# A decoder layer on one core: the columns' load and constants moved behind the first LayerNorm, the table load ahead of the first wait, and three stretches of unread matmuls dropped or cut

## The chip, the cores and the metric

The kernel runs on one NeuronCore of a Trainium2 chip. The metric is the device time of one execution in microseconds (us), lower is better. "PE" is TensorE, "ACT" is ScalarE, "DVE" is VectorE, "POOL" is GpSimd, and "SP" is SyncE, which here only issues transfers.

## The reference

```python
def reference(x, ctx_1024, ...):                      # x, ctx: (32, 128, 256) float32
    x = x + attn(layernorm(x), Wq, bq, Wk, bk, Wv, bv, Wo, bo)   # linear, 16 heads, phi = elu + 1
    x = x + xattn(layernorm(x), ctx, ctx, Wq, Wk, Wv)            # softmax, 16 heads of 16
    x = x + ffn(layernorm(x), w1, w2, h1, h2, w3, ...)           # ternary weights, hidden 1024
    return x

def attn(x, ...):
    q, k, v = phi(x @ Wq.T + bq), phi(x @ Wk.T + bk), x @ Wv.T + bv   # by head
    num = einsum('bhsd,bhsde->bhse', q, cumsum(k[..., :, None] * v[..., None, :], axis=2))
    den = einsum('bhsd,bhsd->bhs', q, cumsum(k, axis=2))
    return (num / (den[..., None] + 1e-6)) @ Wo.T + bo

def ffn(x, ...):
    h = silu(tlin(x, w1_w, w1_s)) * tlin(x, w2_w, w2_s)    # tlin(x, w, s) = (x @ w.T) * s
    h = gelu(tlin(h, h1_w, h1_s)); h = gelu(tlin(h, h2_w, h2_s))
    return tlin(h, w3_w, w3_s)
```

## The kernel before

The 32 sequences are worked on in 16 groups of two (g = 0 to 15, 256 tokens each), and the feed-forward part in 8 blocks of two groups. A planner in Python, run when the program is built, fixes for each engine one list of steps (`ln1T`, `q`, `k`, `xk`, `v`, `xv`, `lin_scores`, and so on); at run time every engine goes through its list in order and waits on semaphores. Nothing in the change alters the planner's tables, so the lists stay as they are.

All transfers of the start are issued by SP on one queue, one behind the other: `x_in` (the first group's input), `cst` (identity, masks), `columns_sb` (38 columns of scales and biases for 128 partitions, 152 bytes to a partition), then the seven weights. After the fifth weight come the context, `bvb`, and then `x_in` for group 1, which waits until the first transposes have read `x_in` (`xn1_turned`); behind it stand `xb`, `bob`, and the weights `woT` and `xqT`.

A weight becomes two parts: ACT copies it to a rounded fp32r part (`split`, L767) and DVE computes the rest (`split`, L934). The first LN1 is: statistics on DVE (L869, L872), the reciprocal root on POOL (`ve`, `rstd`, L706 and L709), normalisation on DVE (L875). PE then transposes the result (`ln1T`, L1058), ACT and DVE split it (L764, L879), and the projections `q` and `k` (L1082, L1087) follow, then `xk`, `v` and `xv` (L1097), where the x stands for the cross attention, which works on the context. ACT takes the exponentials of q and k (L777, L783), DVE makes phi from them (L885, L890), and DVE writes `kz`, k masked by head (L953). PE's `lin_scores` (L1141) needs `kz`; its products are masked on DVE (`lin_mask`, `att_l`, L968) and summed with v on PE (`lin_sums`, L1113); DVE turns the sums (`by_token`, L909) and divides.

The context of a group, `ctx_in`, is rounded by ACT (`ctxs`, L772) and its rest computed by POOL (L734); `xk` of that group waits for both, and ACT's L772 for group 1 waits until `xv` of group 0 is done.

Between these steps PE runs matmuls of the identity with itself, whose results nobody reads. The table FILL says ahead of which step, and how many; they go to the bank that the step will overwrite:

```python
FILL = {("ln1T", 0, 0): 24, ("q", 0, 0): 20, ("xv", 0, 0): 40, ("lin_scores", 0, 1): 20}
```

They need `identb`, the bf16 identity, which ACT makes from `cst` after it has loaded its table of functions (L751, L752).

Of the kernel before, what the change touches and what calls it, by code (L numbers as in the profile page):

```python
# [5 lines left out]
def decoder_layer_program(nc, x, ctxT, wqT, wkT, wvT, woT, bv, bo, xqT, xkT, xvT,  # L6
# [3 lines left out]
    ALU, ACT, AX = mybir.AluOpType, mybir.ActivationFunctionType, mybir.AxisListType  # L10
# [301 lines left out]
    while left:  # L312
        upcoming = []
        for engine in engines:
# [14 lines left out]
            if engine == "tensor" and found:  # L329
# [4 lines left out]
                for entry in found:  # L334
                    step, n = entry[1][1], entry[1][3]
# [27 lines left out]
            if not found:  # L363
                continue
            _, key, when = found[0]
            _, step, g, n = key
            took = tasks[key][1]
            if engine == "tensor":
# [40 lines left out]
    def steps(engine):  # L409
        return [(step, g, n) for _, step, g, n in program[engine]]  # L410
# [13 lines left out]
    def sem(name):  # L424
        return outer.enter_context(nc.semaphore(name))

    with outer:
        flag = outer.enter_context(nc.sbuf_tensor("inexact_flag", [1, 1], I32))
        flag_ready = sem("flag_ready")
        cols = outer.enter_context(nc.sbuf_tensor("columns_sb", [P, 4 * KH + 3 * C], F32))  # L430
        s1c, s2c, sh1c, sh2c = (cols[:, n * KH:(n + 1) * KH] for n in range(4))
        s3c, bqc, bkc = (cols[:, 4 * KH + n * C:4 * KH + (n + 1) * C] for n in range(3))
# [3 lines left out]
        with ctx:  # L436
            def sb(name, shape, dt=F32):
                return ctx.enter_context(nc.sbuf_tensor(name, shape, dt))
# [9 lines left out]
            bq1, bk1 = (sb(n, [P, C]) for n in ("bq1", "bk1"))  # L448
# [17 lines left out]
            v, xv = sb("v", [P, GB, H, 2 * HD]), sb("xv", [P, GB, H, 2 * HD])  # L466
# [22 lines left out]
            s1h, s12 = sb("s1h", [P, KH]), sb("s12", [P, KH])  # L489
# [3 lines left out]
            consts_loaded, cols_loaded = sem("consts_loaded"), sem("cols_loaded")  # L493
            weights = {n: sem(f"{n}_loaded") for n in ("wq", "wk", "wv", "xk", "xv", "wo", "xq", "bv", "bo")}
            ln_const, const_ready, act_const, bias_ready = sem("ln_const"), sem("const_ready"), sem("act_const"), sem("bias_ready")
# [29 lines left out]
            scales = sem("scales_done")  # L525
# [31 lines left out]
            def pbank(step, g, n=0):  # L557
                return bank[place[step, g, n]]

            def wait_pbank(eng, step, g, n=0):  # L560
                if use_before[step, g, n] is not None:
                    wait_freed(eng, *use_before[step, g, n])

            def wait_count(eng, s, count):

                if count > 0:
                    eng.wait_ge(s, count)
# [22 lines left out]
            def _(eng):  # L590
                def load_x(g):
                    wait_count(eng, xn1_turned, g)
                    eng.dma_start(x_in[:, :, :], x[GB * g:GB * g + GB].rearrange("b s d -> s b d")).then_inc(x_loaded, 16)

                def load_xb(g):
                    wait_count(eng, xn2_turned, g)
                    eng.dma_start(xb[:, :, :], x[GB * g:GB * g + GB].rearrange("b s d -> s b d")).then_inc(xb_loaded, 16)

                def load_ctx(g):
                    wait_count(eng, ctx_done, g)  # L600
                    eng.dma_start(ctx_in[:, :, :], ctxT.rearrange("(c p) t -> p c t", p=P)[:, :, T * g:T * g + T])\
                       .then_inc(ctx_loaded, 16)
# [26 lines left out]

                load_x(0)  # L630
                eng.dma_start(cst[:, :], consts).then_inc(consts_loaded, 16)
                eng.dma_start(cols[:, :], columns).then_inc(cols_loaded, 16)
                for n, (dst, src) in enumerate(zip(whole, (wqT, wkT, wvT, xkT, xvT, woT, xqT))):
                    if n == 5:
                        load_ctx(0)
                        eng.dma_start(bvb[:, :], bv.partition_broadcast(P)).then_inc(weights["bv"], 16)
                        load_x(1)
                        load_xb(0)
                        eng.dma_start(bob[:, :], bo.partition_broadcast(P)).then_inc(weights["bo"], 16)
                    eng.dma_start(dst, src.rearrange("(c p) o -> p c o", p=P)).then_inc(weights[SPLIT[n]], 16)  # L640
# [106 lines left out]

            @block.scalar
            def _(eng):
                eng.wait_ge(consts_loaded, 16)  # L750
                eng.preload_act_table(ACT.Exp)  # L751
                eng.activation(identb[:, :], ident, ACT.Copy).then_inc(act_const, 1)  # L752
                eng.wait_ge(cols_loaded, 16)
                eng.activation(s1h[:, :], s1c[:, :], ACT.Copy, scale=0.5).then_inc(scales, 1)
                eng.wait_ge(scales, 1)

                def halves(t):
                    return t[:, :].rearrange("p (c t) -> p c t", c=C)
# [1 line left out]
                for step, g, n in steps("scalar"):  # L760
# [7 lines left out]
                    elif step == "ctx":  # L768
# [2 lines left out]
                        wait_count(eng, xv_psum, g)  # L771
                        eng.activation(ctxs[:, 0, :, :], ctx_in[:, :, :], ACT.Copy).then_inc(ctx_hi, 1)  # L772
                    elif step == "q":
                        eng.wait_ge(q_psum, g + 1)
                        wait_count(eng, kz_done, 2 * g)
                        for c in range(C):
# [89 lines left out]
            def _(eng):  # L866
# [7 lines left out]
                def normalise(ln, which, dst, src, b):  # L874
                    eng.tensor_scalar(dst, src, mv[:, which, b, 0:1], rstd[:, which, b:b + 1], ALU.subtract, ALU.mult)\  # L875
                       .then_inc(ln["xn"], 1)
# [37 lines left out]
                    eng.transpose(out[:, :, :].rearrange("p c (k s) -> p k c s", s=32),  # L914
                                  o[:, :].rearrange("p (k c d) -> p k c d", c=C, d=32)).then_inc(out_turned, 1)

                eng.wait_ge(cols_loaded, 16)
                eng.tensor_scalar(bq1[:, :], bqc[:, :], 1.0, None, ALU.add).then_inc(bias_ready, 1)
                eng.tensor_scalar(bk1[:, :], bkc[:, :], 1.0, None, ALU.add).then_inc(bias_ready, 1)
                eng.scalar_tensor_tensor(s12[:, :], s1c[:, :], 0.5, s2c[:, :], ALU.mult, ALU.mult).then_inc(bias_ready, 1)  # L920
                eng.wait_ge(bias_ready, 3)

                for step, g, n in steps("vector"):
                    if step == "ln1_stats":
# [3 lines left out]
                    elif step == "ln1":  # L928
                        eng.wait_ge(LN1["rstd"], g + 1)
                        for b in range(GB):  # L930
                            normalise(LN1, 0, xn1[:, b, :], x_in[:, b, :], b)
                    elif step == "split":
                        eng.wait_ge(split_hi, g + 1)
                        eng.tensor_tensor(split[g][:, 1, :, :], whole[g], split[g][:, 0, :, :].bitcast(F32), ALU.subtract)\  # L934
# [113 lines left out]
            def _(eng):  # L1048
# [11 lines left out]

                FILL = {("ln1T", 0, 0): 24, ("q", 0, 0): 20, ("xv", 0, 0): 40, ("lin_scores", 0, 1): 20}

                def fill(step, g, n):
                    if (step, g, n) in FILL:
                        first = 4 * n if step in ("lin_scores", "max", "x_scores") else n // 2 if step == "lin_sums" else n
                        wait_pbank(eng, step, g, first)
                        for _ in range(FILL[step, g, n]):
                            eng.matmul(pbank(step, g, first)[:, 0:P], identb[:, :], identb[:, :], start=True, stop=True)  # L1070
# [80 lines left out]
                for step, g, n in steps("tensor"):  # L1151
# [90 lines left out]
                    elif step == "hidden":  # L1242
                        n, quarter = n // 4, n % 4
# [41 lines left out]
        with ctx:  # L1285
# [9 lines left out]
            s1h, s12 = sb("general_s1h", [P, KH]), sb("general_s12", [P, KH])  # L1295
# [244 lines left out]
```

## Time and profile before

| | |
|---|---|
| Median of 3 runs | 1069.11 us (1068.78 to 1071.15) |
| The profiled execution's own time | 1070.74 us |
| Its span in the trace | 1068.9 us |
| PE busy | 1041.0 us, 97% |
| DVE busy | 770.6 us, 72% |
| ACT busy | 528.7 us, 49% |
| POOL busy | 262.1 us, 25% |
| Granted clock of PE over the span | 0.999 |

The page divides the span into 40 slices; PE shows 9 tenths or more in all but the first, where it shows 7. So PE is the engine that the kernel is short of, and the only slice in which it visibly rests is the one that this change is about. A start time in the rows below is counted from the start of the span, and the figure behind it is how long the row lasted.

### The profile page before, as it was taken

Reading aid. Unit: us, or ns where it says so; the run is one execution under the profiler, and the core shown is the slowest. Engines: PE = TensorE matmul, PEld = TensorE weight load, DVE = VectorE, ACT = ScalarE, POOL = GpSimd, SP = SyncE. Lnnn points to the kernel's source line nnn. Section 1 sums busy time; section 2 is a strip of 40 time slices with the busy share of each in tenths; the row PEclk is TensorE's granted clock in tenths of the full one; section 3 lists DMA queues with packets and bytes.
Section 4 is the critical chain, followed back from the end, with each engine's and each line's share of the span. In section 5 each row is a group of like instructions: output and inputs, shape, how many; then the busy total and the mean of one; then the engine's idle time right before and its main releaser. Section 6 shows DMA issues by size and latency. Waiting matters only on the chain.

```text
span 1068.9 us, 25693 instructions
## 1 busy us (share of the span) xinstructions
PE 1041.0 (97%) x10186; PEld 867.0 (81%) x10186; DVE 770.6 (72%) x1708; ACT 528.7 (49%) x855; POOL 262.1 (25%) x363
## 2 busy tenths in 40 slices
PE   7999999999999999999999999999999999999997
PEld 7989877878877888778788878787888888787886
DVE  5999898767996879777898778987688356413321
ACT  4344554855546635555455546374543635333431
POOL 3323352100441115301161011520025002400500
PEclk9999999999999999999999999999999999999999
DMA  5687866443643453543644425453364335545541
GB/s 161 228 285 252 254 230 209 159 138 104 210 148 125 139 166 131 168 136 119 212 137 162 139 86 167 159 147 114 124 231 146 131 125 209 175 142 192 170 155 63
DMA packets 76744, 174.90 MB, mean 164 GB/s; under 512 B 10960, under 2 KB 26448, under 8 KB 76624
## 3 DMA queue, kind: packets, MB, share of 16 engines
q1 hardware_dynamic: 73168, 161.70, 45.1%
q10 hardware_dynamic: 3456, 11.54, 3.9%
q8 instruction: 83, 1.36, 0.5%
q14 instruction: 37, 0.30, 0.1%
HBM read 145.38 MB, written 39.35 MB: 173 GB/s over the span
## 4 chain that ended last, share of the span: by engine, by line
PE 85%; DVE 10%; issue 2%; DMA 2%; ACT 0%; POOL 0%; SPq 0%; ACTq 0%; DVEq 0%
PE bank L1254 43%; PE bank L1141 8%; PE bank L1239 6%; PE bank L1274 6%; PE bank L1113 5%; PE bank L1082 5%; PE bank L1097 3%; PE bank L1087 2%; PE bank L1058 2%; DVE hidden_full L1020 2%; DVE mx L989 1%; DVE hidden_full L1023 1%; PE bank L1191 1%; PE bank L1134 1%; PE bank L1070 1%
## 5 line engine op out<-in xcount | busy, mean ns | idle before, releaser
L1254 PE MATMUL bank<-hidden_a,weight_ring 128*128 128x512 f32 x1024 | 251.4, 396 | 0.0
L1254 PE MATMUL bank<-hidden_b,weight_ring 128*128 128x512 f32 x1024 | 248.0, 395 | 0.3 <-DVE inexact_flag L1045 0.3
L1254 PEld LDWEIGHTS bank<-hidden_b,weight_ring 128*128 128x128 f32 x1024 | 187.7, 188 | 39.4 <-issue 0.8
L1254 PEld LDWEIGHTS bank<-hidden_a,weight_ring 128*128 128x128 f32 x1024 | 187.2, 188 | 40.0 <-issue 1.4
L857 ACT ACTIVATE hidden_full<-bank,columns_sb 128x512 f32<-128x512 f32 x128 | 88.2, 689 | 221.0 <-PE bank L1254 220.6
L706 POOL TENSOR_TENSOR ve<-mv,eps 128x1 f32<-128x1 f32 (+1 forms) x80 | 21.0, 262 | 472.7 <-DVE mv L872 472.7
L1239 PE MATMUL bank<-hidden_b,weight_ring 128*128 128x512 f32 x512 | 123.0, 393 | 1.8 <-DMA weight_ring<-weights_scratch 1.8
L745 POOL TENSOR_TENSOR hidden_a<-hidden_full,hidden_a 128x512 fp32r<-128x512 f32 x64 | 83.1, 1299 | 168.1 <-ACT hidden_a L852 166.9
L1239 PEld LDWEIGHTS bank<-hidden_b,weight_ring 128*128 128x128 f32 x512 | 94.2, 188 | 21.8 <-DMA weight_ring<-weights_scratch 2.2
L1028 DVE TENSOR_TENSOR hidden_a<-hidden_full,hidden_a 128x512 fp32r<-128x512 f32 x64 | 43.6, 683 | 70.4 <-ACT hidden_a L863 70.1
L989 DVE TENSOR_REDUCE mx<-bank 128x4 f32<-128x512 f32 x128 | 80.3, 679 | 16.1 <-PE bank L1141 15.9
L968 DVE TENSOR_TENSOR att_l<-bank,cst 128x512 f32<-128x512 f32 x128 | 80.5, 676 | 9.9 <-PE bank L1141 9.9
L824 ACT ACTIVATE att_x<-bank 128x512 f32<-128x512 f32 x128 | 67.6, 604 | 40.0 <-PE bank L1141 39.8
L1028 DVE TENSOR_TENSOR hidden_b<-hidden_full,hidden_b 128x512 fp32r<-128x512 f32 x64 | 47.3, 743 | 54.3 <-ACT hidden_b L863 54.1
L909 DVE STREAM_TRANSPOSE by_token<-bank 128x512 f32<-128x512 f32 x64 | 45.5, 711 | 39.4 <-PE bank L1113 39.0
L847 ACT ACTIVATE hidden_full<-bank,s1h 128x512 f32<-128x512 f32 x64 | 44.1, 689 | 50.5 <-PE bank L1239 48.7
L730 POOL TENSOR_TENSOR residual<-residual,stats 128x256 f32<-128x256 f32 x64 | 59.3, 949 | 24.4 <-DMA stats<-stats_scratch 23.1
L1274 PE MATMUL bank<-hidden_a,weight_ring 128*128 128x512 f32 x256 | 64.3, 398 | 0.0
L1274 PEld LDWEIGHTS bank<-hidden_a,weight_ring 128*128 128x128 f32 x256 | 46.4, 188 | 9.5 <-issue 0.2
L852 ACT ACTIVATE hidden_a<-hidden_full 128x512 fp32r<-128x512 f32 x64 | 40.2, 628 | 24.8 <-DVE hidden_full L1023 24.6
L1023 DVE SCALAR_TENSOR_TENSOR hidden_full<-bank,s,hidden_full 128x512 f32<-128x512 f32 x64 | 48.1, 751 | 2.3
L709 POOL TENSOR_TENSOR rstd<-ve,mhalf 128x1 f32<-128x1 f32 (+1 forms) x80 | 48.1, 601 | 6.3
(135 smaller groups left out, 1696.5 us busy)
## 6 DMA issues: line engine op xcount, KB each, us to landing
weight_ring<-weights_scratch SPq DMA_DIRECT2D x160, 512.0 KB, 3.8
weights_scratch<-in_h ACTq DMA_DIRECT2D x16, 512.0 KB, 5.0
xn3T_scratch<-hidden_b SPq DMA_DIRECT2D x16, 512.0 KB, 4.3
weight_bits<-in_h SPq DMA_DIRECT2D x32, 256.0 KB, 3.7
weight_ring<-weights_scratch SPq DMA_DIRECT2D x32, 256.0 KB, 2.7
values_scratch<-hidden_full SPq DMA_DIRECT2D x14, 512.0 KB, 4.8
xv<-values_scratch SPq DMA_DIRECT2D x14, 512.0 KB, 4.7
x_in<-in_x SPq DMA_DIRECT2D x16, 256.0 KB, 3.3
```

Of the source, the lines that this page charges most:

```text
L730: last = eng.tensor_tensor(half[:, c], half[:, c], (sd, mean)[n], (ALU.mult, ALU.add)[n])
L745: eng.tensor_tensor(HA[:, 1, n, :], full[:, n % NFULL, :], HA[:, 0, n, :].bitcast(F32), ALU.subtract)\
L824: eng.activation(att_x[:, (NU * g + n) % NX, :, :], pbank("x_scores", g, n)[:, :].rearrange("p (j s) -> p j s", j=4), ACT.Exp, scale=SCALE ...
L857: eng.activation(full[:, (KH + n) % NFULL, :], pbank("hidden", g, n)[:, :], ACT.Gelu, scale=sc).then_inc(h_full, 1)
L968: eng.tensor_tensor(att_l[:, (NU * g + n) % NL, :, :], pbank("lin_scores", g, n)[:, :].rearrange("p (j s) -> p j s", j=4), causal.rearrang ...
L989: eng.tensor_reduce(mx[:, b, 4 * r:4 * r + 4], pbank("max", g, n)[:, :].rearrange("p (j t) -> p j t", j=4), AX.X, ALU.max).then_inc(max_do ...
L1023: eng.scalar_tensor_tensor(f_, pbank("gate", g, 2 * n + 1)[:, :], s12[:, n:n + 1], f_, ALU.mult, ALU.mult)\
L1028: eng.tensor_tensor(dst[:, 1, m, :], full[:, (KH + n) % NFULL, :], dst[:, 0, m, :].bitcast(F32), ALU.subtract)\
L1141: mm = eng.matmul(pbank(step, g, 4 * b + r)[:, j * S:(j + 1) * S], stationary(rows, e, m, b), moving(rows, e, m, b), start=not shifted, st ...
L1239: mm = eng.matmul(pbank(step, g, n)[:, :], ring[:, n // 4, at_:at_ + P], HB[:, part, kk, :], start=(kk == 0 and part == 0), stop=(kk == C ...
L1254: mm = eng.matmul(pbank(step, g, n)[:, :], ring[:, slot, kk * P:(kk + 1) * P], src[:, part, kk, :], start=(kk == 0 and part == 0), stop=(k ...
L1274: mm = eng.matmul(pbank(step, g, c)[:, :], ring[:, slot, kk % 4 * P:(kk % 4 + 1) * P], HA[:, part, kk, :], start=(kk == 0 and part == 0), ...
```

## The change

The load of the columns is issued after the first two weights. ACT loads its table before it waits for `cst`, and makes `s1h` (half of a column scale, read much later by the tanh) only ahead of the first `q`. DVE makes `bq1`, `bk1` and `s12` from the columns after the first LN1's normalisation. Of the unread matmuls, those ahead of `xv` and of the second `lin_scores` are left out, and the others cut from 24 to 22 and from 20 to 14.

```diff
                 load_x(0)
                 eng.dma_start(cst[:, :], consts).then_inc(consts_loaded, 16)
-                eng.dma_start(cols[:, :], columns).then_inc(cols_loaded, 16)
                 for n, (dst, src) in enumerate(zip(whole, (wqT, wkT, wvT, xkT, xvT, woT, xqT))):
+                    if n == 2:
+                        eng.dma_start(cols[:, :], columns).then_inc(cols_loaded, 16)
...
-                eng.wait_ge(consts_loaded, 16)
                 eng.preload_act_table(ACT.Exp)
+                eng.wait_ge(consts_loaded, 16)
                 eng.activation(identb[:, :], ident, ACT.Copy).then_inc(act_const, 1)
-                eng.wait_ge(cols_loaded, 16)
-                eng.activation(s1h[:, :], s1c[:, :], ACT.Copy, scale=0.5).then_inc(scales, 1)
-                eng.wait_ge(scales, 1)
...
                     elif step == "q":
+                        if g == 0:
+                            eng.wait_ge(cols_loaded, 16)
+                            eng.activation(s1h[:, :], s1c[:, :], ACT.Copy, scale=0.5).then_inc(scales, 1)
+                            eng.wait_ge(scales, 1)
                         eng.wait_ge(q_psum, g + 1)
...
-                eng.wait_ge(cols_loaded, 16)
-                eng.tensor_scalar(bq1[:, :], bqc[:, :], 1.0, None, ALU.add).then_inc(bias_ready, 1)
-                eng.tensor_scalar(bk1[:, :], bkc[:, :], 1.0, None, ALU.add).then_inc(bias_ready, 1)
-                eng.scalar_tensor_tensor(s12[:, :], s1c[:, :], 0.5, s2c[:, :], ALU.mult, ALU.mult).then_inc(bias_ready, 1)
-                eng.wait_ge(bias_ready, 3)
+                def biases():
+                    eng.wait_ge(cols_loaded, 16)
+                    ...
+                    eng.wait_ge(bias_ready, 3)
...
                             normalise(LN1, 0, xn1[:, b, :], x_in[:, b, :], b)
+                        if g == 0:
+                            biases()
...
-                FILL = {("ln1T", 0, 0): 24, ("q", 0, 0): 20, ("xv", 0, 0): 40, ("lin_scores", 0, 1): 20}
+                FILL = {("ln1T", 0, 0): 22, ("q", 0, 0): 14}
```

On DVE, at the start of its list, stood this in the kernel before (`stats`, `mv`: LN1's statistics; `x_in` written from itself: the normalisation; `wq`: the rest of the first weight):

```order
L918 TENSOR_SCALAR bq<-columns_sb 128x2
L919 TENSOR_SCALAR bk<-columns_sb 128x2
L920 SCALAR_TENSOR_TENSOR s<-columns_sb 128x8
L869 BN_STATS stats<-x_in 128x6
...
L872 BN_AGGR mv<-stats 128x2
L934 TENSOR_TENSOR wq<-att_x,wq 128x512
L875 TENSOR_SCALAR x_in<-x_in,mv,rstd 128x256 x2
L934 TENSOR_TENSOR wk<-att_x,wk 128x512
```

Now the same place reads:

```order
L871 BN_STATS stats<-x_in 128x6
...
L874 BN_AGGR mv<-stats 128x2
L939 TENSOR_TENSOR wq<-att_x,wq 128x512
L877 TENSOR_SCALAR x_in<-x_in,mv,rstd 128x256 x2
L921 TENSOR_SCALAR bq<-columns_sb 128x2
L922 TENSOR_SCALAR bk<-columns_sb 128x2
L923 SCALAR_TENSOR_TENSOR s<-columns_sb 128x8
L939 TENSOR_TENSOR wk<-att_x,wk 128x512
```

The three column instructions went from the head of the list to a place behind the normalisation, but the first weight's rest still stands between the statistics and the normalisation.

On PE, from the first `k` of the cross attention to the second `lin_scores`, stood this (a row of `identb` is unread matmuls; `att_l,v` is `lin_sums`):

```order
L1087 MATMUL bank<-ctxs,xwk 128x256 x2
L1097 MATMUL bank<-wv,xn1T 128x256 x12
L1070 MATMUL bank<-identb 128x128 x40
L1097 MATMUL bank<-xwv,ctxs 128x256 x12
L1141 MATMUL bank<-qf,kz 128x128 x16
...
L1113 MATMUL bank<-att_l,v 32x128 x16
L1070 MATMUL bank<-identb 128x128 x20
L1141 MATMUL bank<-qf,kz 128x128 x16
```

Now it reads:

```order
L1092 MATMUL bank<-ctxs,xwk 128x256 x2
L1102 MATMUL bank<-wv,xn1T 128x256 x12
L1102 MATMUL bank<-xwv,ctxs 128x256 x12
L1146 MATMUL bank<-qf,kz 128x128 x16
...
L1118 MATMUL bank<-att_l,v 32x128 x16
L1146 MATMUL bank<-qf,kz 128x128 x16
```

Two rows of unread matmuls are gone; each was directly ahead of a step that waits for other engines too.

## Rows read from the trace of the kernel before

**Rows 1.** Chain that ended last, start of the span: start, length, what.
```profile
1.26 2.62 DMA cst<-in_consts
...
3.88 1.28 ACT L751
...
5.63 2.72 PE bank L1070 x24
8.35 0.94 PE bank L1058 x4
9.29 2.05 PE bank L1070 x20
...
17.05 2.25 PE bank L1070 x40
19.30 1.49 PE bank L1097 x12
...
26.93 1.22 PE bank L1070 x20
```

**Rows 2.** Timeline of DVE, first 10 us; in brackets idle time before and its releaser.
```profile
4.68 0.17 DVE L918 TENSOR_SCALAR bq<-columns_sb 128x2 f32<-128x2 f32 x1 [4.68 <-DMA columns_sb<-in_columns]
...
5.02 0.43 DVE L869 BATCH_NORM_STATS2 stats<-x_in 128x6 f32<-128x256 f32 x1
...
7.39 0.73 DVE L875 TENSOR_SCALAR x_in<-x_in,mv,rstd 128x256 f32<-128x256 f32 x2
...
9.96 0.69 DVE L879 TENSOR_TENSOR xn1T<-bank,xn1T 128x512 fp32r<-128x512 f32 x1 [0.63 <-ACT xn1T L764]
```

**Rows 3.** Timeline of POOL, whole start; same columns.
```profile
6.62 0.72 POOL L709 TENSOR_TENSOR rstd<-ve,mhalf 128x2 f32<-128x2 f32 x1
...
22.00 1.30 POOL L734 TENSOR_TENSOR ctxs<-ctx_in,ctxs 128x512 fp32r<-128x512 f32 x1 [4.38 <-ACT ctxs L772]
```

**Rows 4.** Timeline of SP's queue: when a transfer was issued.
```profile
1.76 0.42 SPq L632 DMA_DIRECT2D columns_sb<-in_columns  x1
2.23 0.43 SPq L640 DMA_DIRECT2D att_x<-in_wqT  x1
```

**Rows 5.** DMA issues of the first 16 us: count, KB, us from issue to landing.
```profile
att_x<-in_wqT SPq DMA_DIRECT2D x1, 256.0 KB, 3.8
...
x<-in_woT SPq DMA_DIRECT2D x1, 256.0 KB, 4.3
```

**Rows 6.** Timeline of ACT, first 30 us.
```profile
12.85 0.84 ACT L777 ACTIVATE ex<-bank,columns_sb 128x256 f32<-128x256 f32 x2 [1.37 <-PE bank L1087]
15.11 0.63 ACT L767 ACTIVATE wo<-x 128x512 fp32r<-128x512 f32 x1 [1.41 <-DMA x<-in_woT]
15.64 0.82 ACT L783 ACTIVATE ex<-bank,columns_sb 128x256 f32<-128x256 f32 x2
```

**Rows 7.** Timeline of DVE, 16 to 80 us.
```profile
16.64 0.42 DVE L885 TENSOR_SCALAR ex<-ex 128x512 f32<-128x512 f32 x1
...
19.15 0.88 DVE L953 TENSOR_SCALAR kz<-ex,cst 128x512 f32<-128x512 f32 x2
...
27.00 0.72 DVE L909 STREAM_TRANSPOSE by_token<-bank 128x512 f32<-128x512 f32 x1 [1.97 <-PE bank L1113]
...
72.84 0.42 DVE L980 TENSOR_TENSOR x<-bank,xb 128x256 f32<-128x256 f32 x1 [0.46 <-PE bank L1194]
```

**Rows 8.** Timelines of POOL and DVE, where the two meet.
```profile
35.71 1.29 POOL L734 TENSOR_TENSOR ctxs<-ctx_in,ctxs 128x512 fp32r<-128x512 f32 x1
35.79 1.69 DVE L875 TENSOR_SCALAR x_in<-x_in,mv,rstd 128x256 f32<-128x256 f32 x2
```

**Rows 9.** Timeline of PE: places where it waited.
```profile
23.36 0.50 PE L1087 MATMUL bank<-ctxs,xwk 128*128 128x256 f32 x2 [0.42 <-POOL ctxs L734]
...
43.09 1.17 PE L1141 MATMUL bank<-qf,kz 32*128 32x128 f32 x32 [0.92 <-issue]
...
984.95 9.36 PE L1239 MATMUL bank<-hidden_b,weight_ring 128*128 128x512 f32 x40 [1.79 <-DMA weight_ring<-weights_scratch]
```

More of the change, by code:

```diff
@@ L749, in _ @@
             def _(eng):
+                eng.preload_act_table(ACT.Exp)
                 eng.wait_ge(consts_loaded, 16)
-                eng.preload_act_table(ACT.Exp)
                 eng.activation(identb[:, :], ident, ACT.Copy).then_inc(act_const, 1)
-                eng.wait_ge(cols_loaded, 16)
-                eng.activation(s1h[:, :], s1c[:, :], ACT.Copy, scale=0.5).then_inc(scales, 1)
-                eng.wait_ge(scales, 1)
                 def halves(t):
@@ L915, in turn_and_divide @@
                                   o[:, :].rearrange("p (k c d) -> p k c d", c=C, d=32)).then_inc(out_turned, 1)
-                eng.wait_ge(cols_loaded, 16)
-                eng.tensor_scalar(bq1[:, :], bqc[:, :], 1.0, None, ALU.add).then_inc(bias_ready, 1)
-                eng.tensor_scalar(bk1[:, :], bkc[:, :], 1.0, None, ALU.add).then_inc(bias_ready, 1)
-                eng.scalar_tensor_tensor(s12[:, :], s1c[:, :], 0.5, s2c[:, :], ALU.mult, ALU.mult).then_inc(bias_ready, 1)
-                eng.wait_ge(bias_ready, 3)
+                def biases():
+                    eng.wait_ge(cols_loaded, 16)
+                    eng.tensor_scalar(bq1[:, :], bqc[:, :], 1.0, None, ALU.add).then_inc(bias_ready, 1)
+                    eng.tensor_scalar(bk1[:, :], bkc[:, :], 1.0, None, ALU.add).then_inc(bias_ready, 1)
+                    eng.scalar_tensor_tensor(s12[:, :], s1c[:, :], 0.5, s2c[:, :], ALU.mult, ALU.mult).then_inc(bias_ready, 1)
+                    eng.wait_ge(bias_ready, 3)
                 for step, g, n in steps("vector"):
```

## The prediction

> **What bounds the kernel now.** I read the page first: PE is busy for 97% of the span, and only the first slice shows it resting. So the second view was the chain of work that ended last, in order of time, over the first 60 us [rows 1]. It is on PE almost throughout, and before 30 us it has four stretches of L1070, the unread matmuls: 2.72, 2.05, 2.25 and 1.22 us. The reader is to see that these look like time that can be had back, 8.2 us in all, and that this is only so where nothing else would have held PE. The third view was the timeline of each engine over the same time, where the brackets tell what each idle engine waited for. DVE rests for the last time at 27.00, where it waits for `lin_sums`; from there to 72.4 it has work without a break [rows 7], and PE waits instead, for 0.92 us at 43.09 [rows 9]. That sets the measure of everything below: the change is worth what it moves the DVE row at 27.00. Later both engines hand the lead to each other, and no time in the program is absolute, so a shift there should reach the end.
>
> **Change part by part.**
>
> *The table load.* ACT waits for `cst` until 3.88, loads for 1.28 us, and only then copies `identb`; PE starts at 5.63 [rows 1]. With the load ahead of the wait it falls into idle time, the copy starts at 3.90, and PE starts at 5.63 - 1.28 = 4.35.
>
> *LN1.* The statistics could not start before 5.02, because the columns' three instructions, waiting for a landing at 4.68, stood ahead [rows 2]. From 5.02 to the end of `rstd` at 7.34 [rows 3] are 2.32 us. `x_in` is the first transfer and `cst`, issued behind it, has landed at 3.88, so the statistics start by 3.9 and `rstd` is there by 6.2. This is no longer what counts: the rest of `wq` stands between statistics and normalisation. `wqT` was issued at 2.23 and landed 3.8 us later, at 6.03 [rows 4, 5]; from there to the normalisation at 7.39 are 1.36 us of copy and rest. It now takes the columns' place at 1.76. With the same 3.8 it lands at 5.56. The columns are 128 pieces of 152 bytes ahead of it in the queue; if they held it up besides, it lands earlier, and I bound that by 0.35 us, which is less than a whole issue (0.42). So LN1 is normalised from 6.57 to 6.92 on and done 0.73 later, at 7.3 to 7.65, against 8.12.
>
> *The transposes.* 22 unread matmuls at 2.72/24 = 0.113 us each end at 6.85, so PE waits 0.5 to 0.8 us for LN1 before the transposes. They begin at 7.35 to 7.7 and, with 0.94 as before, end at 8.3 to 8.65 against 9.29. That is a shift of 0.65 to 1.0; I take 0.8. The columns' three instructions, 0.3 us on DVE behind the normalisation, cost nothing: DVE waited 0.63 us there for ACT [rows 2], and without that cover they would cost their 0.3. `s1h`, a copy of 8 columns, is at most the 0.4 us that one of the two q exponentials of 256 takes, on ACT in a wait of 1.37 us for q [rows 6]; equally free.
>
> *q to xv.* 14 unread matmuls at 2.05/20 give 1.45 us, so q begins at 9.95 instead of 9.29 + 2.05 = 11.34: a shift of 1.4. Nothing on PE waited between there and 17.05, so v ends at 15.65, and without the 40 matmuls `xv`, 1.49 us, ends at 17.15 instead of 19.30 + 1.49 = 20.79 [rows 1].
>
> *Where the 2.25 us go.* `lin_scores` needs `kz`. Follow it back: `kz` ended at 19.15 + 0.88 = 20.03; the chain ahead of it on DVE starts with L885 at 16.64 [rows 7], which needs ACT's k exponential, done at 16.46, which stands in ACT's list behind the copy of `wo`, which waited 1.41 us for the transfer of `woT` [rows 6]. That transfer is issued behind the `x_in` of group 1, which waits for the transposes, and takes 4.3 us [rows 5]. So this chain moves by the transposes' 0.8, not by PE's 1.4, and DVE's slack of 0.15 adds to it: `kz` ends at 19.1. PE will stand idle from 17.15 to 19.1, almost all that the 40 matmuls had filled. `lin_scores` moves from 20.79 to 19.1, by 1.7. Behind it, `xk` of group 1 waited 0.42 us for POOL's `ctxs` [rows 9]; that chain (ACT's `xv` copy, L772, L734) now ends near 19.8, well ahead, so the wait goes and with it some of the slow matmuls about it: 0.4 to 0.65, I take 0.5. DVE's row at 27.00 moves by 2.2.
>
> *What comes late next.* POOL's `ctxs` rest, 1.30 us from 22.00 [rows 3], moves to about 18.5 to 19.8, because its ACT chain follows the k exponential too. Before, it lay beside masking from PSUM. Now it lies beside `kz` and group 1's normalisation, 18.2 to 19.9 on DVE. What that does is seen elsewhere: two normalisations took 1.69 us beside POOL [rows 8] where the first group's took 0.73 [rows 2], ending only after POOL's instruction had. If the second `kz` half is caught, it ends about 0.8 later, and `lin_scores` with it; if only the normalisation is caught, the transposes of group 1 wait some 0.3. I charge 0.4, between the two. The Trainium skill (SBUF — State Buffer, the reading of its diagram) says that VectorE and GpSimd share one port pair as an exclusive lock, so that the loser blocks for the whole instruction. The trace agrees (1.69 against 0.73); without that rule the sum would be 2.2, with it between 1.4 and 1.9.
>
> *The last stretch*, 1.22 us at 26.93, is worth nothing: behind 27.00 DVE leads, and PE's 0.92 wait at 43.09 becomes 2.1.
>
> Sum: 0.8 + 0.15 + 0.75 (PE was that much later than `kz`) + 0.5 - 0.4 = 1.8 us. Against the profiled execution's own 1070.74 (its span is 1068.9) that makes 1068.9, but this execution lay 1.6 above the median of the runs shown; against 1069.11 it makes 1067.3.
>
> **Rivals.**
> 1. *No clash with POOL, or `wqT` lands early.* The sum is then 2.2 to 3.1: 1066.0 to 1066.9. For it: POOL's start depends on three ACT instructions, and 0.1 us decides who is first. Against it: either DVE instruction is in POOL's way.
> 2. *The gain is lost on the way.* Either the clock rises later still (it has a rest of 0.8 us and fewer matmuls to go by), so that PE itself brings `kz` late: a rise at 13 costs 1.5 on PE and leaves 0.7; or DVE and POOL meet more often between 27 and 72. Gain 0 to 1.2: 1067.9 to 1069.1.
> 3. *Slower: the clock falls in the new rest.* PE will rest 1.9 to 2.7 us from 17.15, after a short start. From `lin_scores` to the end of `lin_sums` it has 5.5 us of work; at half speed that is up to 5.5 more. From 1.8 us of it at the low clock on, the change loses; at worst it gives 1069.1 + 3.7 = 1072.8. Against it: after a rest of 1.79 us at 984.95, matmuls of 512 columns went on at 9.36/40 = 0.234 each [rows 9], the fast pace. But that was after long work, and the rest will be longer. The Trainium skill (TensorE: Matmul & The Clock Gate, What's actually happening) says that throttled is the default state and activity is what lifts it; by that rule leaving out filler ahead of a rest speaks for this rival, and the four rows of L1070 are the trace's only witness.
>
> **How the numbers follow.** Forecast, gain 1.3 to 2.2: 0.45. Rival 1: 0.27. Rival 2: 0.18. Rival 3: 0.10. Two tenths of a per cent, 2.1 us, is about what a measurement of this kernel tells from no change (the three runs span 2.4). Faster by more is rival 1 and the upper quarter of the forecast: 0.39; slower by more is rival 3 and a little: 0.11; the rest, 0.50, lies within. The range runs from rival 1's 1065.9 to rival 2's end with the runs' scatter, 1069.4, and leaves out rival 3 and the tails.
>
> **What would show it.** `identb` near 3.9 and the first L1070 near 4.35; the normalisation near 6.7; transposes near 7.5 with PE idle some 0.6 before; `wo` on ACT near 14.3; PE idle about 1.9 us before the first `lin_scores` near 19.1 to 19.9; `by_token` near 25.2 with DVE busy behind it; and a POOL `ctxs` row that overlaps a long `kz` or `x_in` row. I am wrong if matmuls behind 17 us take the slow pace, or if the row at 25.2 has moved but the end has not.

## The result, and the profile after

| | before | after |
|---|---|---|
| Median | 1069.60 us (16 executions) | 1075.15 us (16 executions, 1072.67 to 1079.16) |
| Profiled execution, its span | 1070.74, 1068.9 | 1075.01, 1073.2 |
| Granted clock of PE, mean over the span | 0.999 | 0.995 |
| PE busy | 1041.0 | 1042.5 |

The change makes the kernel slower: after to before is 1.0044, 95% interval 1.0032 to 1.0055, or 4.7 us where 1.8 of gain were forecast. Rival 3, which had a chance of 0.10, is what happened, and it happened twice; the median lies above even its worst case, 1072.8.

First the granted clock. This is PE in the stretches about the two rests in the kernel after; the columns are the stretch, its length, PE's busy time with its instructions, the granted clock, DMA's share and GB/s.

```profile
17.00:19.00 2.00, 0.84 (x8) 1.00 0.00 0
19.00:21.00 2.00, 1.17 (x32) 1.00 0.00 0
21.00:22.00 1.00, 0.86 (x5) 0.51 0.27 71
22.00:23.00 1.00, 1.00 (x7) 0.50 0.59 192
23.00:24.00 1.00, 1.00 (x7) 0.50 0.45 90
24.00:25.00 1.00, 1.00 (x8) 0.78 0.49 172
...
44.00:45.00 1.00, 0.64 (x20) 0.96 0.92 375
45.00:46.00 1.00, 1.00 (x21) 0.50 0.81 271
46.00:47.00 1.00, 1.00 (x5) 0.50 0.19 66
47.00:48.00 1.00, 1.00 (x6) 0.50 0.00 1
48.00:49.00 1.00, 1.00 (x9) 0.84 0.00 0
```

Twice the pace halves, from 2.4 to 1.2 GHz, for 3.4 us each time. Adding up what is missing from 1.00 gives 0.49 + 0.50 + 0.50 + 0.22 = 1.7 us in the first and 0.04 + 3 x 0.50 + 0.16 = 1.7 in the second.

Now PE's own timeline of the kernel after; a bracket is how long PE was idle ahead of the row, and for what.

```profile
4.24 2.50 PE L1075 MATMUL bank<-identb 128*128 128x128 bf16 x22 [4.24 <-ACT identb L753]
7.95 1.12 PE L1063 MATMUL bank<-cst,x_in 128*128 128x128 f32 x4 [1.20 <-DVE x_in L877]
8.86 1.70 PE L1075 MATMUL bank<-identb 128*128 128x128 bf16 x14
10.31 0.93 PE L1087 MATMUL bank<-xn1T,wq 128*128 128x256 f32 x4
...
16.27 1.57 PE L1102 MATMUL bank<-xwv,ctxs 128*128 128x256 f32 x12
19.57 1.17 PE L1146 MATMUL bank<-qf,kz 32*128 32x128 f32 x32 [1.73 <-issue]
21.14 1.12 PE L1063 MATMUL bank<-cst,x_in 128*128 128x128 f32 x4 [0.40 <-DVE x_in L877]
21.91 1.20 PE L1087 MATMUL bank<-ctxs,xwk 128*128 128x256 f32 x4
...
38.18 0.72 PE L1087 MATMUL bank<-ctxs,xwk 128*128 128x256 f32 x4
...
44.36 1.63 PE L1146 MATMUL bank<-qf,kz 32*128 32x128 f32 x32 [2.49 <-issue]
```

The same four matmuls of `xk` take 1.20 us at 21.91 and 0.72 at 38.18. The rests ahead of the two `lin_scores` are 1.73 and 2.49 us; before, PE had filler ahead of the first and rested 0.92 at the second [rows 9].

The other engines of the kernel after, DVE, ACT and POOL, in the same columns, at the rows that answer to [rows 2, 3, 6, 7]:

```profile
6.55 0.69 DVE L939 TENSOR_TENSOR wq<-att_x,wq 128x512 fp32r<-128x512 f32 x1 [1.89 <-ACT wq L765]
7.16 0.73 DVE L877 TENSOR_SCALAR x_in<-x_in,mv,rstd 128x256 f32<-128x256 f32 x2
...
19.39 1.70 DVE L877 TENSOR_SCALAR x_in<-x_in,mv,rstd 128x256 f32<-128x256 f32 x2
...
27.20 0.72 DVE L911 STREAM_TRANSPOSE by_token<-bank 128x512 f32<-128x512 f32 x1 [3.13 <-PE bank L1118]
...
42.34 1.92 DVE L958 TENSOR_SCALAR kz<-ex,cst 128x512 f32<-128x512 f32 x2
...
5.89 0.63 ACT L765 ACTIVATE wq<-att_x 128x512 fp32r<-128x512 f32 x1 [1.79 <-DMA att_x<-in_wqT]
...
14.68 0.63 ACT L765 ACTIVATE wo<-x 128x512 fp32r<-128x512 f32 x1 [1.55 <-DMA x<-in_woT]
...
5.09 0.71 POOL L710 TENSOR_TENSOR rstd<-ve,mhalf 128x2 f32<-128x2 f32 x1
...
19.07 1.54 POOL L735 TENSOR_TENSOR ctxs<-ctx_in,ctxs 128x512 fp32r<-128x512 f32 x1 [2.00 <-ACT ctxs L770]
...
42.40 1.57 POOL L735 TENSOR_TENSOR ctxs<-ctx_in,ctxs 128x512 fp32r<-128x512 f32 x1 [4.29 <-ACT ctxs L770]
```

`by_token`, on which the sum was put, comes at 27.20 with 3.13 us of idle DVE ahead of it, where 27.00 and 1.97 stood [rows 7]: the early start is gone by then. The last two POOL rows each run beside a DVE row that takes twice its usual time.

One of the 16 executions had a mean clock of 0.999, as before, and was the shortest, 1072.67 us. It has no trace, but it suggests that a part of the loss against 1069.60 stays without a fall of the clock.

### The profile page after: what moved, and what is told of

The parts are those of the page before. It is cut to its first block, busy times and chain, and to the rows that moved or that the text cites. A ratio compares the mean times of both kernels' runs of the same rounds, so it can differ in the third digit from the quotient of the medians.

```text
span 1073.2 us, 25557 instructions
## 1 busy us (share of the span) xinstructions
PE 1042.5 (97%) x10118; PEld 866.7 (81%) x10118; DVE 774.4 (72%) x1708; ACT 528.2 (49%) x855; POOL 262.4 (24%) x363
## 4 chain that ended last, share of the span: by engine, by line
PE 80%; DVE 12%; issue 3%; DMA 3%; ACT 1%; POOL 0%; SPq 0%; ACTq 0%; DVEq 0%
PE bank L1259 43%; PE bank L1146 8%; PE bank L1279 5%; PE bank L1118 5%; PE bank L1244 5%; PE bank L1087 4%; PE bank L1102 3%; PE bank L1092 2%; PE bank L1063 2%; DVE hidden_full L1025 2%; DVE mx L994 2%; DVE hidden_full L1028 1%; DMA weight_ring<-weights_scratch 1%; PE bank L1196 1%; PE bank L1139 1%
## 5 line engine op out<-in xcount | busy, mean ns | idle before, releaser
L1244 PEld LDWEIGHTS bank<-hidden_b,weight_ring 128*128 128x128 f32 x512 | 94.2, 188 | 21.4 <-DMA weight_ring<-weights_scratch 1.9
L731 POOL TENSOR_TENSOR residual<-residual,stats 128x256 f32<-128x256 f32 x64 | 59.0, 944 | 25.5 <-DMA stats<-stats_scratch 24.3
```

The source lines that it names most:

```text
L731: last = eng.tensor_tensor(half[:, c], half[:, c], (sd, mean)[n], (ALU.mult, ALU.add)[n])
L1244: mm = eng.matmul(pbank(step, g, n)[:, :], ring[:, n // 4, at_:at_ + P], HB[:, part, kk, :], start=(kk == 0 and part == 0), stop=(kk == C ...
```

## The experiments

Twelve kernels, all run in the same manner beside the kernel before, profiled once each. Their results together; "rest 1" and "rest 2" are PE's idle time in the profiled execution right ahead of the first `lin_scores` of group 0 (near 20 us) and of group 1 (near 44), "low" means that the granted clock fell to 0.5 behind it.

| kernel | median us | ratio to before (95%) | rest 1 | rest 2 |
|---|---|---|---|---|
| after | 1075.15 | 1.0044 (1.0032 to 1.0055) | 1.73 low | 2.49 low |
| head_only | 1070.99 | 1.0011 (0.9998 to 1.0023) | 0.50 | 0.87 |
| fills_only | 1076.23 | 1.0056 (1.0041 to 1.0070) | 2.87 low | 2.57 low |
| xv_back | 1072.67 | 1.0024 (1.0010 to 1.0039) | none | 2.57 low |
| ls_back | 1071.98 | 1.0015 (1.0003 to 1.0026) | 3.08 low | 0.96 |
| both_back | 1069.76 | 0.9982 (0.9971 to 0.9994) | none | 0.94 |
| rests_filled | 1071.60 | 1.0010 (0.9999 to 1.0020) | 1.10 | 0.35 |
| start_long | 1070.56 | 0.9991 (0.9977 to 1.0005) | 2.90 low | 0.78 |
| no_meeting | 1074.01 | 1.0033 (1.0022 to 1.0045) | 2.01 | 2.48 |
| half_fills | 1070.53 | 0.9998 (0.9984 to 1.0012) | 0.69 | 2.37 low |
| norm_first | 1066.57 | 0.9965 (0.9951 to 0.9979) | none | 0.95 |
| weights_late | 1064.95 | 0.9951 (0.9933 to 0.9970) | 1.19 | 0.85 |
| kz_free | 1070.39 | 1.0000 (0.9989 to 1.0011) | none | none |

**The change in two halves.** head_only has the change's loads and order with the unread matmuls of before; fills_only has the old order with the changed table.

```diff
 # head_only, against the kernel after
-FILL = {("ln1T", 0, 0): 22, ("q", 0, 0): 14}
+FILL = {("ln1T", 0, 0): 24, ("q", 0, 0): 20, ("xv", 0, 0): 40, ("lin_scores", 0, 1): 20}
 # fills_only, against the kernel before
-FILL = {("ln1T", 0, 0): 24, ("q", 0, 0): 20, ("xv", 0, 0): 40, ("lin_scores", 0, 1): 20}
+FILL = {("ln1T", 0, 0): 22, ("q", 0, 0): 14}
```

> The changed kernel with all four stretches of unread matmuls as before (24, 20, 40, 20); only the loads and constants are moved. Theory A (the clock falls in rests that the unread matmuls had filled): no stretch below a granted clock of 1.00 behind the first 12 us, DVE's first by_token at 25.5 to 26.5 instead of 27.20, and 1 to 2 us below the kernel before, near 1068. Theory B (what was lost is lost to POOL: PE runs ahead, POOL's rest of the context comes earlier and blocks kz and the normalisation): the earlier start alone still brings these meetings, and the time is 2 us or more above the kernel before.

> The kernel before with only the unread matmuls changed (22, 14, none, none). Theory A: the rest ahead of the first lin_scores is about 1.5 to 2 us and that ahead of the second group's lin_scores about 2 us, the granted clock reads 0.5 behind at least one of them, and the time is 3 to 6 us above before. Theory B: no clock below 1.00, kz of the second group about 1.9 us, the time 1 to 3 us above.

The loss is all in the table: with it alone the kernel takes 1.0056, with the rest alone 1.0011. In fills_only the clock is low from 24.1 to 27.5 and from 48.0 to 51.5. But head_only did not bring the gain of 1 to 2 us that was expected of it. Its trace has no fall before PE's last work, and `by_token` is at 28.02, not at 25.5 to 26.5: PE rests 1.22 us ahead of the transposes, the slow pace lasts to about 13.4, and `kz` begins at 21.33, where it began at 19.15 before.

**Each stretch put back.** The three entries keep 22 and 14 and add one or both of the others.

```diff
-FILL = {("ln1T", 0, 0): 22, ("q", 0, 0): 14}
+FILL = {("ln1T", 0, 0): 22, ("q", 0, 0): 14, ("xv", 0, 0): 40}                              # xv_back
+FILL = {("ln1T", 0, 0): 22, ("q", 0, 0): 14, ("lin_scores", 0, 1): 20}                      # ls_back
+FILL = {("ln1T", 0, 0): 22, ("q", 0, 0): 14, ("xv", 0, 0): 40, ("lin_scores", 0, 1): 20}    # both_back
```

> The changed kernel with the 40 unread matmuls ahead of xv put back. Theory A: the low clock from 21.0 to 24.3 goes, the one from 45.0 to 48.3 stays; by_token near 25.5, and of the 5.5 us lost some 2 come back: 1072 to 1073.5. Theory B: these 40 stand well before the meeting at 42.3, which stays; no more than 0.5 us comes back.

> The changed kernel with the 20 unread matmuls ahead of the second lin_scores put back. Theory A: the rest ahead of lin_scores of the second group falls from 2.5 to some 1.3 us, the clock stays up there, while the first low stretch at 21.0 remains: 1071 to 1073. Theory B: PE is 1.2 us later in front of POOL's rest, kz of the second group is back at 0.9 us, and all of the loss but 1 us is gone, whatever the clock does.

> The changed kernel with both later stretches (40 ahead of xv, 20 ahead of the second lin_scores) put back, the first two left at 22 and 14. Theory A (each low stretch costs on its own): neither the clock at 21 nor that at 45 falls, both parts come back, 1070 to 1071, level with the kernel before. If the first two stretches mattered for the falls, one of them is still there and the time stays at 1072 or more.

Each of the first two removes one of the two low stretches and leaves the other. With both back the change is a gain of 0.18%, 1.9 us. That it is the size of the forecast is luck: two of the forecast's terms, 0.75 and 0.5, came from `xv` without the 40 matmuls, which stand here again. Nor does the trace show where the gain arises: the transposes begin at 8.26 (8.18 before), and `by_token` is at 26.91, 0.09 ahead of before. The 20 matmuls that the prediction held to be worth nothing are worth 1.0044 - 1.0015, 3.1 us, when put back alone. ls_back changes two things near 44 us at once, though: the clock holds, and `kz` takes 0.88 where it took 1.92. So it does not tell these two apart. Its rest 1 is 3.08 where after has 1.73, and 1.0 of that is another `kz`, the first one: it took 1.88 us (19.11) beside POOL's `ctxs` (19.31).

**Only the rests filled.** Unread matmuls are put where PE rests, ahead of the two `lin_scores`, where none had stood.

```diff
+FILL = {("ln1T", 0, 0): 22, ("q", 0, 0): 14, ("lin_scores", 0, 0): 32, ("lin_scores", 1, 0): 40}
```

> The changed kernel with unread matmuls where its trace shows PE resting: 32 behind xv, directly ahead of the first lin_scores (rest of 1.73 us), and 40 directly ahead of the second group's first lin_scores (rest of 2.49 us); none ahead of xv and of the second lin_scores. Theory A: they stand in time that is lost anyway, the clock holds through both places, and xv with POOL's chain behind it is early: 1067.5 to 1069.5, below the kernel before. Theory B: the meetings with POOL are as in the changed kernel (kz of the second group 1.9 us), so 1.5 us or more of the loss stays: 1072 or more.

No clock falls behind them, and 3.6 us come back (1.0044 to 1.0010), about the 3.4 that the low rows add up to. The trace shows it directly: from the first `lin_scores` to `by_token` are 5.57 us here (21.63 to 27.20) and 7.63 in after (19.57 to 27.20), where 0.40 of it is PE's wait for the long normalisation. The time, 1071.6, lies between what the two theories had expected. For 1.0010 is not 0.9982: something besides the clock was lost. In this trace both `kz` are long, the first (19.59) with 1.94 us and the one near 42 with 2.01.

**A longer start.** More matmuls at the start, so that the first rise of the pace comes sooner and no rest stands ahead of the transposes.

```diff
+FILL = {("ln1T", 0, 0): 34, ("q", 0, 0): 20, ("xv", 0, 0): 40, ("lin_scores", 0, 1): 20}
```

> The changed kernel with 34, 20, 40 and 20 unread matmuls: all of the kernel before, and 10 more in the new rest of 1.2 us ahead of the first transposes. Theory A': with only the old numbers the clock first rose at 13.3 instead of 11.1, because of that rest, and this ate the earlier start; now PE works without a rest from 4.3 on, the first rise is at or before 11, and the time is 1 to 2 us below the same kernel with 24: 1068 to 1069.5. Rival: the first rise comes when it comes, whatever PE did in that rest, and the time is as with 24 (1071).

The start went as meant, with the fast pace from about 7.9 us (the transposes at 8.06 took 0.66 us, where after has 1.12), and yet the clock fell behind rest 1, and stayed low for 6.8 us, twice as long as elsewhere. Two thirds of that rest are a transfer's, and the last 1.0 us is POOL's. ACT, DVE and POOL in this run:

```profile
10.81 0.20 ACT L774 ACTIVATE s1h<-columns_sb 128x8 f32<-128x8 f32 x1
11.52 0.84 ACT L779 ACTIVATE ex<-bank,columns_sb 128x256 f32<-128x256 f32 x2 [0.51 <-PE bank L1092]
16.36 0.63 ACT L765 ACTIVATE wo<-x 128x512 fp32r<-128x512 f32 x1 [4.00 <-DMA x<-in_woT]
16.89 0.82 ACT L785 ACTIVATE ex<-bank,columns_sb 128x256 f32<-128x256 f32 x2
...
20.27 1.92 DVE L958 TENSOR_SCALAR kz<-ex,cst 128x512 f32<-128x512 f32 x2
...
20.61 1.28 POOL L735 TENSOR_TENSOR ctxs<-ctx_in,ctxs 128x512 fp32r<-128x512 f32 x1 [4.39 <-ACT ctxs L770]
```

k's exponential stands behind the copy of `wo`, and `woT` took 6.2 us here (4.3 before [rows 5]). PE had finished the filler and `xv` long before and waited for `kz`, which took 1.92 us beside POOL's `ctxs`. Its twelve times fall apart into six from 1068.14 to 1069.35 and six from 1071.76 to 1073.04, the profiled one among the latter, with mean clocks of 0.998 to 0.999 in the first and 0.996 to 0.998 in the second.

**POOL kept out of the first normalisation's way.** In the kernel after, POOL's `ctxs` of group 1 (19.07) runs beside group 1's normalisation (19.39, 1.70 us).

```diff
                     elif step == "ctx":
                         eng.wait_ge(ctx_hi, g + 1)
+                        if g == 1:
+                            eng.wait_ge(LN1["xn"], 2 * GB)
```

> The changed kernel, but POOL's rest of the context of group 1 waits until DVE has normalised that group. Theory A: x_in's normalisation is back at 0.73 us and the 0.40 us rest ahead of the transposes goes, but the rest of 1.73 us ahead of lin_scores and the two low stretches stay: 1074 to 1075.5, at most 0.8 us better. Theory B: this meeting starts the loss: 1072 or less.

The normalisation takes 0.73 us again (20.09). The median gains 1.2 us (1.0044 to 1.0033), and the intervals overlap. Its profiled execution, with 1071.99 the lowest of the twelve, shows no fall of the clock behind rests of 2.01 and 2.48; the other eleven go up to 1076.62 with mean clocks of 0.995 to 0.997. They have no traces, but by these means one and the same rest seems to be followed by a fall in most executions, and not in all.

**Half of the filler.**

```diff
+FILL = {("ln1T", 0, 0): 22, ("q", 0, 0): 14, ("xv", 0, 0): 20, ("lin_scores", 0, 1): 10}
```

> The changed kernel with half of what it left out: 20 unread matmuls ahead of xv and 10 ahead of the second lin_scores. The rests of PE ahead of the two lin_scores should be 1.1 and 0.6 us shorter than in the changed kernel, so about 0.7 and 1.9 us. Theory (a rest of the length seen there, 1.7 to 3.1 us, lets the pace fall; a short one does not): the first stretch at the low clock (21 to 25 us) does not come, the second, behind a rest of 1.9, may; 1070.5 to 1073. Rival (it is the number of matmuls left out, or the short start, not the rest, that counts): both stretches stay and the time is within 1 us of the changed kernel's 1075. If both are gone, the time is about that with both put back whole, 1069.8.

Rest 1 shrinks to 0.69 and the clock holds there. Rest 2 stays long, since DVE leads there and `kz` is late (1.90 us beside POOL), and the clock falls.

**The normalisation ahead of the first weight's rest.** On top of both_back, DVE's list has its normalisation in front of the rest of `wq`.

```diff
-                for step, g, n in steps("vector"):
+                dve_steps = list(steps("vector"))
+                early = next(t for t in dve_steps if t[0] == "ln1" and t[1] == 0)
+                dve_steps.remove(early)
+                at = next(i for i, t in enumerate(dve_steps) if t[0] == "split")
+                dve_steps.insert(at, early)
+                for step, g, n in dve_steps:
```

(`biases()` moves from the normalisation to behind the first `split`.)

> The changed kernel with 40 and 20 unread matmuls put back, and on DVE the first LN1's normalisation ahead of the rest of wq instead of behind it (the columns' three instructions stay behind wq's rest). If the transposes waited for wq's transfer by way of that rest, as I now read it, the normalisation starts near 5.6 instead of 7.5, the transposes near 6.9 instead of 8.3 with no rest before them, and everything to the first lin_scores moves by what woT's landing allows, 0.5 to 1.3 us: 1068.5 to 1069.5, ratio 0.997 to 0.998. Rival: as in the run with a longer start, woT lands no earlier though it is issued earlier, kz stays near 19.3 and the rest ahead of lin_scores becomes long enough for the pace to fall: 1070.5 to 1072.

The gain is larger than expected. DVE and PE in this kernel:

```profile
5.94 0.73 DVE L877 TENSOR_SCALAR x_in<-x_in,mv,rstd 128x256 f32<-128x256 f32 x2 [1.17 <-POOL rstd L710]
6.62 0.69 DVE L942 TENSOR_TENSOR wq<-att_x,wq 128x512 fp32r<-128x512 f32 x1
...
25.07 0.72 DVE L911 STREAM_TRANSPOSE by_token<-bank 128x512 f32<-128x512 f32 x1 [1.95 <-PE bank L1123]
...
6.73 1.12 PE L1068 MATMUL bank<-cst,x_in 128*128 128x128 f32 x4
```

The normalisation no longer waits for `wqT`, in this kernel or in the next (5.94 and 5.86). The transposes follow the 22 matmuls without a rest, and `by_token` is at 25.07, 1.9 ahead of before.

**`wo` and `xwq` out of the way.** As norm_first, and the copies and rests of these two weights stand behind group 1's `ctxs` on ACT and behind group 1's normalisation on DVE. The 40 matmuls ahead of `xv` are left out again, the 20 stay.

```diff
+                late = [t for t in act_steps if t[0] == "split" and t[1] in (5, 6)]
+                act_steps = [t for t in act_steps if t not in late]
+                at = next(i for i, t in enumerate(act_steps) if t[0] == "ctx" and t[1] == 1)
+                act_steps[at + 1:at + 1] = late
...
-FILL = {("ln1T", 0, 0): 22, ("q", 0, 0): 14, ("xv", 0, 0): 40, ("lin_scores", 0, 1): 20}
+FILL = {("ln1T", 0, 0): 22, ("q", 0, 0): 14, ("lin_scores", 0, 1): 20}
```

> As norm_first, and besides the copies and rests of wo and xwq stand behind the context copy of group 1 on ACT and behind group 1's normalisation on DVE, and the 40 unread matmuls ahead of xv are left out (the 20 ahead of the second lin_scores stay). Theory (PE's rest ahead of the first lin_scores is ACT waiting for woT in front of k's exponential): ACT's k exponential starts right behind q's, kz ends near 17, lin_scores follows xv near 17.3 with a rest under 0.6 us, and there is no low clock behind it; by_token moves from 27.2 to about 25, the end to 1067 to 1068.5. Rival A (leaving out the 40 lets the pace fall by itself): a low clock near 20 to 24 us though the rest is short, 1070 to 1073. Rival B (POOL or the masks are late next): kz early, by_token within 0.5 us of 27, 1069 to 1070.

ACT, PE and DVE in this kernel:

```profile
13.09 0.84 ACT L790 ACTIVATE ex<-bank,columns_sb 128x256 f32<-128x256 f32 x2 [1.47 <-DVE qf L897]
...
14.59 1.52 PE L1116 MATMUL bank<-xwv,ctxs 128*128 128x256 f32 x12
17.30 1.17 PE L1160 MATMUL bank<-qf,kz 32*128 32x128 f32 x32 [1.19 <-issue]
...
23.35 0.72 DVE L916 STREAM_TRANSPOSE by_token<-bank 128x512 f32<-128x512 f32 x1 [0.33 <-PE bank L1132]
```

The 40 matmuls are gone, the rest is 1.19, and the clock stays at 1.00. So the filler can go where the rest that it leaves is short. The transfer is the smaller part of what moved `kz` from 17.57 to 16.33: in norm_first `kz` began 5.69 us behind DVE's first `ex` row, 0.26 more than where DVE had no break, and here 4.68, since the rests of `wo` and `xwq` no longer stand between. `by_token` is at 23.35, 3.65 ahead of before. The median is 1064.95, the best of all and 2 us under the lower end of what was expected, 4.9 us under that of the kernel before in the same comparison (1069.81); the profiled execution, 1068.03, was the longest of the six.

**POOL kept out of `kz`'s way.** In all six kernels without the 20 matmuls (after, fills_only, xv_back, rests_filled, no_meeting, half_fills, which has 10) the two `kz` halves near 42 us took 1.89 to 2.01 us beside POOL's `ctxs`; in all seven that have the 20, before included, they took 0.88. The last run is rests_filled with one wait more on POOL.

```diff
                     elif step == "ctx":
                         eng.wait_ge(ctx_hi, g + 1)
+                        if g == 4:
+                            eng.wait_ge(kz_done, 4)
```

> The run with both rests filled (32 and 40 unread matmuls ahead of the two lin_scores of group 0's and group 1's first use), and besides POOL's context rest of group 4 waits until both kz halves of group 1 are written. In all six kernels that left out the 20 unread matmuls ahead of the second lin_scores, these two kz halves took 1.9 to 2.0 us beside POOL, and in all seven that have the 20 they took 0.88. Theory (the 20 kept PE and ACT late enough that POOL came behind kz; leaving them out lets POOL in first): kz is 0.88 again near 42.3, PE reaches lin_scores 0.6 to 1.0 us sooner, and the time is 0.5 to 1.0 us under that of the run with both rests filled (1071.6 there, 1.0010 of before): ratio 1.0000 to 1.0006. Rival (the DVE pair is long for another reason, or POOL's delay costs as much in xk of group 4): ratio 1.0010 again.

First ACT, DVE and POOL of the kernel before at this place:

```profile
42.01 0.62 ACT L772 ACTIVATE ctxs<-ctx_in 128x512 fp32r<-128x512 f32 x1
...
42.11 0.88 DVE L953 TENSOR_SCALAR kz<-ex,cst 128x512 f32<-128x512 f32 x2
...
42.71 1.41 POOL L734 TENSOR_TENSOR ctxs<-ctx_in,ctxs 128x512 fp32r<-128x512 f32 x1 [4.83 <-ACT ctxs L772]
```

And DVE and POOL in kz_free:

```profile
41.75 0.88 DVE L960 TENSOR_SCALAR kz<-ex,cst 128x512 f32<-128x512 f32 x2
...
42.77 1.30 POOL L737 TENSOR_TENSOR ctxs<-ctx_in,ctxs 128x512 fp32r<-128x512 f32 x1 [5.26 <-DVE kz L960]
```

`kz` is short again, and the ratio goes from 1.0010 to 1.0000. The intervals of the two overlap, so the row shows the mechanism and the median its likely size. The two traces also differ in the first `kz` (0.88 us at 19.56 here, 1.94 at 19.59 there), which the added wait does not touch: POOL began 0.49 us behind it here and 0.36 there.

## Why the prediction was wrong

**The table load and the copy of `identb`** were right: `identb` at 3.79 and the first L1075 at 4.24, against 3.9 and 4.35.

**LN1 was mis-sized.** The wait for `wqT` was named rightly as what remains, but the transfer, issued at 1.76 instead of 2.23, was waited for until 5.89: it took 4.1 us where it had taken 3.8 [rows 5], and landed 0.2 earlier. The normalisation moved from 7.39 to 7.16, not to 6.57 to 6.92, and the transposes ended 0.2 us earlier (9.07, before 9.29) instead of 0.8. Neither "with the same 3.8" nor an earlier landing held. Even the 0.2 is within the scatter of single executions: in the twelve kernels that issue `wqT` at 1.76, ACT's copy of it began between 5.82 and 6.82; in the two that issue it at 2.23, at 6.12 and 6.30. norm_first shows what it hid: the normalisation could start at 5.94.

**`kz`** came out near, but not through `woT`. `wo` was copied at 14.68 (forecast 14.3), `kz` ended at 19.46 (19.1), and `lin_scores` began 1.2 us earlier than before (1.7 forecast). PE's rest ahead of it is 1.73 against 1.9. What set `kz` was DVE's own list: from its first `ex` row, which needs q's exponential, it worked without a break to `kz`, 13.72 to 19.15 before and 13.16 to 18.59 now, 5.43 us both times. So `kz` moved by the 0.56 of q's exponential, which the late LN1 held back. `woT` was close behind (DVE's second `ex` row at 16.08, k's exponential done at 16.04) and led clearly only in start_long.

**The meeting with POOL** came as the milder of the two cases: the normalisation was caught (1.70 us), `kz` was not, and PE waited 0.40 ahead of the transposes, against 0.3 in that case and 0.4 charged. The dearer case came in fills_only, ls_back, rests_filled and start_long, where the first `kz` took 1.88 to 1.94 us.

**The step that failed is the clock**, in two places. The sum had no term for it. Rival 3 described the first rest, its length and the slow matmuls behind it, and priced it too high for one place (up to 5.5 us; the low rows cost 1.7) and too unlikely. What was held against it, the row at 984.95 where 1.79 us of rest were followed by the fast pace, was a single row. The rows after show the granted clock at 0.50 at 22 us and again at 45. The Trainium skill, as quoted for the rival (TensorE: Matmul & The Clock Gate, What's actually happening: throttled is the default state and activity is what lifts it), agrees with them, and had been weighed as less than the one row.

**The second place was not seen at all.** "PE's 0.92 wait at 43.09 becomes 2.1" stood in the prediction, and behind it "worth nothing". The arithmetic was near: 0.92 plus the 1.22 of filler is 2.1, and 2.49 were found. But the same reasoning that made the first rest a risk held here, and no one asked. Besides, with the filler gone ACT reached its `ctxs` copy at 41.70 instead of 42.01, and POOL began 0.06 us behind the start of `kz` (42.40 and 42.34) instead of 0.60 (42.71 and 42.11), so `kz` took 1.92 where it had taken 0.88. In the first two `kz` of all fourteen traces the pair took 1.88 to 2.01 us wherever POOL's `ctxs` began 0.03 to 0.36 us behind it, and 0.87 or 0.88 where POOL began 0.48 us behind or later. Where POOL began ahead of the third `kz`, near 68 us, the pair took 1.82 to 1.92 (0.07 to 0.16 us ahead) or 1.00 to 1.35 (0.62 to 0.96 ahead). The Trainium skill (SBUF — State Buffer, the reading of its diagram) has whichever of VectorE and GpSimd starts first hold their shared port pair for its whole instruction. The rows of after agree: the pair ended at 44.26, 0.3 us behind the end of POOL's row at 43.97.

**The account.** By the ratios, each times 1070 us: the change with both later stretches left in gains 1.9 us (both_back). Leaving out both later stretches costs 6.6, from 0.9982 to 1.0044. Of that, 3.6 is the low clock (filled rests take it away; the intervals lie apart), and about 1.1 the `kz` meeting near 42 us (kz_free takes it away; the intervals overlap). The remaining 1.9, from kz_free to both_back, is not shown. It may be smaller than it looks: the two intervals overlap a little (0.9989 to 1.0011, 0.9971 to 0.9994), and the profiled execution of kz_free has the shorter span of the two, 1068.3 against 1069.0. One candidate stands in the traces: the third `kz` took 1.82 us beside POOL in kz_free (65.77) and 0.88 in both_back (66.23), so that kz_free, 0.46 us ahead there, is 0.48 behind at the next `nshift` row (70.09 and 69.60). It is long in after too (68.30, 1.92), and no run frees it.

## What to carry to other kernels

Unread matmuls ahead of a wait are not idle time that can be had back. Before dropping them, find the rest that PE will then have and what ends it; first shorten that wait, then drop the filler, as weights_late did. An engine that now arrives 0.3 us earlier may meet another one: look at which POOL row will lie beside which DVE row. Look for work in an engine's list that stands ahead of what the critical chain needs, above all where it waits for a late transfer. Moving it away in two places gave about 1.8 and 1.5 us here (the ratio went from 0.9982 to 0.9965, and to 0.9951, where the 40 matmuls went too); the intervals of neighbours overlap, those of the first and the last do not. And one trace is one execution: a transfer issued at the same time began to be used 1 us earlier or later.

## What the runs showed of the hardware

- Behind rests of 1.73, 2.37, 2.49, 2.57 (twice), 2.87, 2.90 and 3.08 us the granted clock fell to 0.5. Once PE had reached the fast pace, it did not behind any rest up to 1.60, nor behind six from 1.71 to 1.88 (1.79 [rows 9]; 1.71, 1.72, 1.78 and 1.88 at the same place near 985 us in rests_filled, start_long, head_only and kz_free; 1.82 at 122.13 in ls_back), nor behind 2.01 and 2.48 (no_meeting). So in this range a rest makes a fall possible and does not decide it.
- Seven of the eight low stretches lasted 3.4 us and cost 1.7; the one in start_long lasted 6.8, from 21.4 to 28.3. A stretch need not begin with PE's first matmul behind the rest: in after `lin_scores` at 19.57 still took its usual 1.17 us.
- The granted clock also falls to 0.5 over the last microseconds of every trace, when PE has finished (before: PE ends at 1062.1, the clock falls at 1065.8). The mean clock holds this too and is not a count of falls that cost time.
- The granted clock does not show the slow pace of the start. The rows of the kernel after read 1.00 up to 21 us, while the 14 unread matmuls at 8.86 took 1.70 us, 0.121 each, against 2.25/40 = 0.056 in [rows 1]. The durations have to be read there.
- The first rise of the pace came between about 7 us (weights_late, where the 14 unread matmuls at 7.36 took 0.94 us) and 14.1 (xv_back), which alone can hide a microsecond of what a change does to the start.
